# Shift rows sent as two transfers of 16 pieces, and the output matrix made earlier, in a one-core attention and MoE kernel

## The reference

```python
q = (x @ wq).reshape(Bq, Tq, N_KV, N_REP, HEAD_DIM)
k = jnp.einsum('bkhl,ld->bkhd', (x @ wk_down).reshape(...), wk_up)
v = jnp.einsum('bkhl,ld->bkhd', (x @ wv_down).reshape(...), wv_up)
scores = jnp.einsum('bqhrd,bkhd->bhrqk', q, k) * scale      # causal mask, softmax
y = jnp.einsum('bhrqk,bkhd->bqhrd', probs, v).reshape(...) @ wo

x = x + _layernorm(attention(_layernorm(x)))
x = x + _layernorm(moe(_layernorm(x)))      # 32 experts, top 6, a shared expert, 16 anchor experts
```

## Time and profile before

| | us |
|---|---|
| median of 3 runs | 396.92 (394.61 to 398.63) |
| the profiled execution | 394.98 |
| its span, first to last instruction | 393.2 |
| PE busy | 374.4 (95%) |
| POOL busy | 284.0 (72%) |
| DVE busy | 277.7 (71%) |
| ACT busy | 237.8 (60%) |
| mean granted clock of TensorE | 0.988 |

### The profile page before, as it was taken

How to read it: one execution, slowest core, us unless ns; L and a number is a source line. 1 busy time by engine, 2 the same in 40 slices (tenths; PEclk the granted TensorE clock), 3 DMA queues, 4 the chain that set the end, 5 groups by cost and what they waited for, 6 DMA issues and landing times.

```text
span 393.2 us, 6898 instructions
## 1 busy us (share of the span) xinstructions
PE 374.4 (95%) x2088; PEld 257.5 (65%) x2088; DVE 277.7 (71%) x707; ACT 237.8 (60%) x475; POOL 284.0 (72%) x336
## 2 busy tenths in 40 slices
PE   7989899999999998999999999999999999999992
PEld 7665455555555554455468887788878888788861
DVE  5979599986876983547348866759766677567674
ACT  4558566774745475844865556856565555665652
POOL 6126768299888799796597884899838997486651
PEclk9989899999999999999999999999999999999998
DMA  7299915805005005000000000000000000000000
GB/s 227 42 213 164 155 43 147 99 2 75 10 0 83 2 1 84 1 3 3 1 3 0 3 0 0 2 28 1 2 0 2 27 2 0 2 8 20 0 1 28
DMA packets 12691, 14.56 MB, mean 37 GB/s; under 512 B 1520, under 2 KB 9136, under 8 KB 12656
## 3 DMA queue, kind: packets, MB, share of 16 engines
q1 hardware_dynamic: 12096, 13.36, 18.1%
q10 hardware_dynamic: 560, 0.77, 0.6%
HBM read 6.26 MB, written 1.05 MB: 19 GB/s over the span
## 4 chain that ended last, share of the span: by engine, by line
PE 71%; POOL 11%; DVE 5%; issue 5%; DMA 3%; ACT 2%; POOLq 0%; ACTq 0%; DVEq 0%
PE ps L1342 11%; PE ps L1343 10%; PE ps L1344 10%; POOL probs L887 8%; PE ps L1442 7%; PE ps L1542 5%; PE ps L1460 5%; PE ps L1543 5%; PE ps L1544 5%; PE ps L1473 4%; PE ps L1483 3%; PE ps L1493 1%; DMA raw<-in_attn_wq 1%; PE ps L1445 1%; DMA qst<-shift_rows 1%
## 5 line engine op out<-in xcount | busy, mean ns | idle before, releaser
L960 POOL TENSOR_TENSOR silu<-silu,cwb 128x512 f32<-128x512 f32 x80 | 102.6, 1295 | 34.4 <-ACT silu L1113 30.3
L1239 DVE TENSOR_REDUCE nmax_h<-ps 128x1 f32<-128x512 f32 (+3 forms) x152 | 91.5, 654 | 30.5 <-PE ps L1445 15.8
L1083 ACT ACTIVATE probs<-ps 128x512 f32<-128x512 f32 (+1 forms) x152 | 78.4, 583 | 45.8 <-PE ps L1460 27.3
L887 POOL TENSOR_TENSOR probs<-probs 128x1024 f32<-128x1024 f32 (+3 forms) x56 | 92.4, 1671 | 16.1 <-PE ps L1473 12.1
L1113 ACT ACTIVATE silu<-ps 128x512 f32<-128x512 f32 x80 | 47.7, 598 | 47.4 <-PE ps L1344 41.4
L1306 DVE TENSOR_TENSOR ps<-silu,ps 128x512 f32<-128x512 f32 (+1 forms) x84 | 57.7, 693 | 24.3 <-POOL silu L960 23.5
L1313 DVE TENSOR_TENSOR h_lo<-ps,h_hi 128x512 fp32r<-128x512 f32 (+1 forms) x84 | 56.8, 685 | 25.5 <-ACT h_hi L1125 25.1
L1342 PE MATMUL ps<-xT_hi,w_hi 128*128 128x512 f32 x164 | 65.4, 399 | 0.0
L1442 PE MATMUL ps<-kst,qst 96*128 96x512 f32 (+3 forms) x192 | 63.9, 399 | 1.1 <-DVE nmax_h L1239 0.4
L1343 PE MATMUL ps<-xT_lo,w_hi 128*128 128x512 f32 x164 | 64.3, 392 | 0.0
L1460 PE MATMUL ps<-qst,kst 98*128 98x512 f32 (+1 forms) x152 | 60.4, 443 | 3.9 <-DMA qst<-shift_rows 3.2
(11 more groups left out here) (190 smaller groups left out, 495.9 us busy)
## 6 DMA issues: line engine op xcount, KB each, us to landing
qst<-q_hi SPq DMA_DIRECT2D x14, 256.0 KB, 5.4
qst<-q_lo SPq DMA_DIRECT2D x7, 256.0 KB, 6.9
x_sb<-in_attn_x SPq DMA_DIRECT2D x4, 256.0 KB, 6.3
raw<-in_ffn_w_gate SPq DMA_DIRECT2D x5, 192.0 KB, 4.8
raw<-in_ffn_w_up SPq DMA_DIRECT2D x5, 192.0 KB, 7.2
raw<-in_ffn_w_down SPq DMA_DIRECT2D x5, 192.0 KB, 3.5
kst<-k_hi SPq DMA_DIRECT2D x6, 128.0 KB, 7.1
result<-x_sb SPq DMA_DIRECT2D x3, 256.0 KB, 2.3
```

The lines of the kernel that those rows point to most:

```text
L887: nc.gpsimd.tensor_tensor(into, into, probs[:, BUF[n, kt], j:end, cols], ALU.add).then_inc(added, 1)
L960: nc.gpsimd.tensor_tensor(silu[:, k % HRING, :], silu[:, k % HRING, :], cwb[:, m % 2, t // ET, :], ALU.mult).then_inc(scaled_ready, 1)
L1083: nc.scalar.activation(probs[:, BUF[n, kt], j:j + w, at:at + cols], bank(full)[:, 0:w * cols].rearrange("p (w c) -> p w c", w=w), ACT.Exp) ...
L1239: nc.vector.tensor_reduce(nmax_h[:, n % 2, i, j:j + w, h], bank(full)[:, 0:w * keys].rearrange("p (w k) -> p w k", w=w), AX.X, ALU.max, ne ...
```

## The change

Four numbers of the planner are changed, and the two shift rows are sent by two transfers, one for each row, each of 16 pieces of 128 numbers (512 bytes). What waits for them waits for both. `am2` and `m_copy` get a lower rank, so that they are placed earlier.

```diff
@@ -160,10 +160,10 @@
-SEED, WOBBLE = 49, 0.04
+SEED, WOBBLE = 8, 0.04
 PE_DEPTH = 17
 DMA_START = 200
-DMA_TIME = {"q_hi_dma": 390, "q_dma": 195, "q_far_dma": 195, "k_hi_dma": 170, "k_dma": 85, "s_dma": 15, "load": 90, "store": 80, "tail_store": 40}
+DMA_TIME = {"q_hi_dma": 390, "q_dma": 195, "q_far_dma": 195, "k_hi_dma": 170, "k_dma": 85, "s_dma": 65, "load": 60, "store": 80, "tail_store": 40}
@@ -287,8 +287,8 @@
-    step("PE", ("am2",), 60, 1.78, ("late_in",), bank=1, until=("m_copy",))
-    step("ACT", ("m_copy",), 45, 1.78, ("am2",))
+    step("PE", ("am2",), 60, 1.0, ("late_in",), bank=1, until=("m_copy",))
+    step("ACT", ("m_copy",), 45, 1.0, ("am2",))
@@ -353,7 +353,7 @@
-        step("ACT", ("s_dma", n), 70, n + 0.9, ("shift_copy", n))
+        step("ACT", ("s_dma", n), 130, n + 0.9, ("shift_copy", n))
@@ -1061,14 +1061,16 @@
-                        act.wait_ge(shift_in[(n - 2) % QRING], 16 * ((n - 2) // QRING + 1))
+                        act.wait_ge(shift_in[(n - 2) % QRING], 16 * SHIFTS * ((n - 2) // QRING + 1))
...
-                    act.dma_start(qst[QROWS:KROWS, n % QRING, :, :].bitcast(F32), shift_rows[:, n % 2, :].bitcast(F32)).then_inc(shift_in[n % QRING], 16)
+                    for a in range(SHIFTS):
+                        row = qst[QROWS + a:QROWS + a + 1, n % QRING, :, :].bitcast(F32).rearrange("a j (i q) -> a (j i) q", q=P)
+                        act.dma_start(row, shift_rows[REP * TPC * a:REP * TPC * (a + 1), n % 2, :].bitcast(F32)).then_inc(shift_in[n % QRING], 16)
@@ -1452,7 +1454,7 @@
-                    pe.wait_ge(shift_in[n % QRING], 16 * (n // QRING + 1))
+                    pe.wait_ge(shift_in[n % QRING], 16 * SHIFTS * (n // QRING + 1))
```

## The result

The changed kernel takes 408.34 us (median of 4 runs, 407.64 to 410.56), against 397.77 us for the kernel before, run beside it. The ratio is 1.028, with a 95% interval of 1.020 to 1.037: the change makes the kernel slower. The profiled execution has a span of 405.8 us, 12.6 more than the 393.2 of the earlier trace rows.

What follows compares the result with a forecast made beforehand. PE was taken as the bound, 95% busy, with a few waits deciding the result. The terms summed to -0.1 us, 394.9 us in the profiled execution's terms; 396.8 us was predicted against the median of 396.92, range 393.0 to 400.5.

Steps and rivals of the forecast that it cites:

- Landing of the shift rows: Shift transfer under load: lands 4.3 to 4.7 us after issue, nearly unchanged from 4.68; at worst 5.3 us.
- Wait at block 1: PE's wait for shift rows at block 1: falls from 1.69 to about 1.1 us, -0.6 us.
- Block 5: PE's wait for shift rows at block 5: one more `p1` ahead of it, -0.5 of 1.55 us.
- The slow stretch: Lowered PE clock behind the block 1 wait, costing about 1.7 us: left as it is.
- Opening: First block: weight tiles ahead of `v_copy` 0 and `shift_copy` 0 on ACT delay `kproj` 1, +0.9 us, bounds 0 and +2.6.
- Extra issues on ACT: ACT's queue: second shift issue per block may delay exponentials and POOL's adds, +0.4 us, bounds 0 and 5.1.
- Switches on PE: Narrow `pv` and `ones` matmuls on PE: 35 runs instead of 33, +0.4 us.
- POOL's add at block 2: PE's 0.6 us wait for POOL's add at block 2: two `p2` and a `pv` ahead of it, -0.3 us.
- Start of the MoE part: Start of the MoE part: `ones` 7 ahead of `g` 1 and `u` 1 hides the `post_out` 3 wait, -0.4 us.
- Rival 2: Shift transfer gets short over 16 engines; both waits and the slow stretch vanish, 4.9 us, giving 393.3 us; chance 0.20.
- Rival 3: Opening: late second weight load doubles PE's pause and grants the slow stretch twice, +4.2 us, 401.1 us; chance 0.14.
- The sign that was named as proof of an error: Anywhere on PE: an idle time over 1 us at a place not named would show the forecast wrong.

Runs made afterwards that it cites:

- filled pauses: Changed kernel with 15 and 9 useless matmuls put into PE's pauses ahead of the shift-row waits at blocks 1 and 5; 401.00 us, ratio 1.014.
- q last: Q of block 3 issued behind the last weight pieces, of block 7 behind block 5's shift rows: kernel before 395.06 and 396.08 us, changed kernel 396.36 us.
- rows first: Q of block 3 issued behind k of chunk 2, of block 7 behind block 5's shift rows: changed kernel 403.09 us, kernel before 397.57 us.
- opening mended: Changed kernel with q of blocks 3 and 7 issued later, and ACT's order in the opening as before; 397.24 us.

## Why the prediction was wrong

The prediction said 396.8 us and no change that can be measured. The place was right, the sign of the term for the shift rows was not.

- **Landing of the shift rows, taken as 4.3 to 4.7 us, "nearly unchanged, since the load ahead of it stays".** This step failed. The load ahead did not stay. Before, one q_hi transfer of 256 KB stood ahead of the rows; after, q_hi twice and q_lo. The prediction counted what stands between `shift` 1 and the wait, and not what stands ahead of `shift` 1: in the new order the last `p2` of block 0, which frees q's place in the ring, is 2.58 us ahead of it instead of 0.66. So q_lo of block 3 is issued at 39.75, ahead of both rows (40.95 and 41.49), where before it came at 41.09 behind the rows at 39.44. DVE's swap of `q_lo` 3 and `nm_split` 1, which the prediction did read, is not what did it: before, SP issued q_lo 2.6 us after DVE had finished it. And the second issue, counted as 0.64 us, lets one q transfer more slip in between even without a new order (412.14 us with the split alone). The rows landed at 7.0 us, outside the upper bound of 5.3. In the Trainium skill (DMA: Bandwidth & Descriptors), the section "Queues, rings and completion order" says that an engine's signal waits for its earlier writes in every queue. The traces agree in part: the second row of block 1 lands 0.2 us behind q_lo in after, and with the split alone each row lands 0.5 us behind the q_hi issued last ahead of it; but the first row of after landed 1.2 us ahead of a q_lo that was issued 1.2 us before it, so the order of issue alone doesn't tell the landing. The prediction had quoted this as speaking against the change and given it no price of its own.
- **Wait at block 1, 1.69 to 1.1 us, -0.6.** It became 3.77. The cover came out right, 3.8 us forecast, 3.74 measured (`shift` 1 at 40.50, PE idle from 44.24), by two slips that cancel: three `p1` of block 2 went ahead of `shift` 1, not two, and three others came behind it, not two. Only the landing was wrong. **Block 5, -0.5**: it went from 1.55 to 2.26 us, by the second issue: with the single transfer in the new order it was 0.61, so the new order did shorten the wait, though the stage from 5 to 6 took 0.7 us more than before.
- **The slow stretch, "I leave it as it is", 1.7 us.** This was the mis-sized term that decides. A stretch was priced as if it always lasted 3.4 us. Behind 3.77 us of idle PE it lasted 20.5, behind 2.26 us 6.9, and together they cost about 8 us (filled pauses), where the one of before cost 1.1 by its second trace and not 1.7. The text had a warning in its own rows, one wait of 1.69 with a stretch and one of 1.55 without: a price that hangs on such a step needs a range in both directions.
- **Opening, +0.9.** Right in mechanism and nearly in size. `w_hi` 0 0 began at 24.27 (said 23.4), `v_copy` 0 behind it, and the first matmul of `kproj` 1 came at 26.50, 1.16 us behind the earlier trace rows; the rows of block 0 were issued at 26.39 us, 0.75 later. The mend of this place gained nothing: PE then met the rows of block 0, in a longer stretch of half clock.
- **Extra issues on ACT, +0.4.** Not seen as such: in the stage from 2 to 5, where three of them lie, after is 0.2 us faster. With q last in the kernel before, the split cost 1.6 us in that stage, where another queue's issue fell between the two, and a wait of 0.98 us at block 6. **Switches on PE, +0.4**: no run takes them by themselves.
- **POOL's add at block 2, -0.3.** It fell from 0.58 to 0.26 us: right.
- **Start of the MoE part, -0.4.** The wait for `post_out` 3 went, but one of 1.30 us for `cwb_copy` came, with 3.4 us of half clock: +1.1 in the stage. The forecast looked at what the order took away there, and not at what the first matmuls of the gate wait for in the new order.
- **Rivals.** Rival 2 priced both waits and the stretch at 4.9 us; taking them out of the kernel before (q last) gave 2 us of span. Rival 3 had the right kind of loss (waits doubled, slow stretch granted again) in the wrong place, and too small, since its stretches were 1.7 us each. No rival put the rows behind more of q, although the change adds an issue behind which SP may step in. The sign that was named as proof of an error, an idle time of over 1 us at a place not named, occurred: `cwb_copy`.

## What to carry to other kernels

A small transfer that an engine waits for is worth what stands ahead of it in the DMA queues when its last piece is issued, on every issuing engine and not only on its own: write down the issue times of all large transfers around it, before and after, and see which pairs change places. Splitting such a transfer makes its last piece later by an issue and by whatever another queue issues in between, so look first whether the large transfer can go later, which here took a few lines and gave back 12 us. When a step moves in one engine's order, look also at what it releases: here a `p2` that moved ahead released q's transfers sooner. Price a new pause of TensorE by the half-clock stretch behind it, with a range, and not by its own length.

## What the runs showed of the hardware

The single transfer of 16 KB landed 2.3 to 2.9 us behind its issue with the queues clear, 4.5 to 4.7 us when one 256 KB transfer had been issued ahead of it, and 6.30 us behind three. Of the two of 8 KB each took 1.8 to 1.9 us with clear queues in most blocks, 3.9 to 4.7 us behind one large transfer, 5.5 to 5.9 behind two (block 5 of after and block 1 with the split alone), and 5.6 to 6.5 us behind three. So the form gave no shelter from the neighbours. By the packets of ACT's queue (34 a block before, 64 after) it did change. Twice the second row came late with nothing else issued: 3.2 us at block 6 of after (a wait of 0.58 us) and 3.6 us at block 5 with the split alone and q last.

How long the clock stays at 1.2 GHz is not a function of the pause alone in these traces:

| wait of PE ahead, us | where | half clock, us |
|---|---|---|
| 3.77, 3.43, 3.06 | block 1 of after, split alone, order alone | 20.5 each |
| 3.29 | block 5, split alone | 6.8 |
| 3.29 | block 1's work at 57.8, rows first | 10.2 |
| 2.26 | block 5 of after | 6.9 |
| 2.21 | block 0, split alone | 10.2 |
| 1.69 | block 1 of before | 3.4 |
| 1.61, 1.55, 1.55 | blocks 1 and 5 of before, two traces | 0 |
| 1.30 | for `cwb_copy`, after; opening mended | 3.4; 0 |
| 0.61 | for DVE, matmuls behind the wait; filled pauses | 10.2; 0 |
| 0.55 | at 54.41, before with rows first | 3.4 |
| under 0.2 | at 52.4, split alone and q last | 6.8 |

In the changed kernel, with the split alone and in the new order alone, the clock rose during or just behind the first run of 16 `probs` by `v_sb` matmuls (63.51 to 66.60 us in after), and in the work ahead of it, many short scores with masks, it did not. Sixteen matmuls put right behind the wait brought it back within 3.4 us. What rule joins these was not tested. PE's idle time was the cause at blocks 1 and 5, which the filled pauses show.
